# Flamingo block on one core: who splits the query weights in the prologue, and when ScalarE loads its sigmoid table

## The reference

```python
q = (layernorm(x) @ Wq.T) * scale;  k = ctx @ Wk.T;  v = ctx @ Wv.T
scores = sigmoid(q . k) per head;   o = (scores @ v) @ Wo.T
x = x + tanh(g_xattn[0]) * o
h = gelu(layernorm(x) @ w1 + b1);   y = h @ w2 + b2        # per expert
x = x + tanh(g_ffn[0]) * y
```

## Time and profile before

| | us |
|---|---|
| median of 3 runs | 1730.21 |
| lowest and highest | 1726.27, 1733.91 |
| profiled execution, own time | 1730.66 |
| its span in the profile | 1729.0 |
| PE busy | 1697.4 |
| DVE busy, ACT busy, POOL busy | 690.2, 776.6, 210.3 |

### The profile page before, as it was taken

How to read it: one execution, slowest core, us unless ns; L and a number is a source line. 1 busy time by engine, 2 the same in 40 slices (tenths; PEclk the granted TensorE clock), 3 DMA queues, 4 the chain that set the end, 5 groups by cost and what they waited for, 6 DMA issues and landing times.

```text
span 1729.0 us, 34127 instructions
## 1 busy us (share of the span) xinstructions
PE 1697.4 (98%) x12442; PEld 1498.7 (87%) x12442; DVE 690.2 (40%) x1171; ACT 776.6 (45%) x1007; POOL 210.3 (12%) x303
## 2 busy tenths in 40 slices
PE   6999999999999999999999999899999999999999
PEld 6888888888888888888888888799999999999998
DVE  5323323323324224233133132455555464655553
ACT  5545545446445455455454454433333333334332
POOL 1111212112111112122121121000000000000000
PEclk9999999999999999999999999999999999999999
DMA  8767767676777677677676676545262535435351
GB/s 262 217 185 218 209 193 204 202 206 204 190 211 211 187 210 215 183 210 211 193 219 193 197 207 198 155 153 175 95 221 98 196 119 174 141 127 176 101 181 58
DMA packets 199674, 315.75 MB, mean 183 GB/s; under 512 B 25368, under 2 KB 152672, under 8 KB 199520
## 3 DMA queue, kind: packets, MB, share of 16 engines
q1 hardware_dynamic: 176176, 236.05, 48.3%
q0 software_dynamic: 23344, 77.68, 12.8%
HBM read 235.06 MB, written 78.58 MB: 181 GB/s over the span
## 4 chain that ended last, share of the span: by engine, by line
PE 91%; DMA 4%; ACT 2%; DVE 1%; issue 1%; SPq 1%; POOLq 0%; ACTq 0%; DVEq 0%
PE fill_ps L539 37%; PE scores_ps L704 18%; PE fill_ps L685 13%; PE scores_ps L571 9%; PE heads_ps L585 8%; PE heads_ps L685 5%; ACT probs L742 2%; DMA k_scr<-k_stage 1%; DMA ctx_raw<-ctxT_in 1%; PE fill_ps L644 0%; SPq L312 0%; DMA xnT<-stat_scr 0%; DMA q_scr<-q_stage 0%; DMA probs<-WKT_in 0%; PE scores_ps L539 0%
## 5 line engine op out<-in xcount | busy, mean ns | idle before, releaser
L742 ACT ACTIVATE probs<-scores_ps 125x1792 f32<-125x1792 f32 x192 | 320.1, 1667 | 110.0 <-PE heads_ps L585 66.2
L539 PE MATMUL fill_ps<-ctx_hl,wK 128*128 128x250 f32 x2304 | 310.6, 284 | 9.3 <-DVE wK L901 8.4
L704 PE MATMUL scores_ps<-ctx_hl,wK 128*128 128x448 f32 x1536 | 316.7, 362 | 0.4 <-ACT st_row L771 0.4
L539 PEld LDWEIGHTS fill_ps<-ctx_hl,wK 128*128 128x128 f32 x2304 | 284.5, 191 | 32.1 <-issue 28.8
L704 PEld LDWEIGHTS scores_ps<-ctx_hl,wK 128*128 128x128 f32 x1536 | 288.0, 188 | 20.5 <-issue 0.8
L539 PE MATMUL fill_ps<-wV,ctx_hl 128*125 128x512 f32 x1152 | 286.8, 398 | 0.0
L539 PEld LDWEIGHTS fill_ps<-wV,ctx_hl 128*125 128x125 f32 x1152 | 208.9, 186 | 49.9
L685 PE MATMUL fill_ps<-wQ,wV 128*128 128x448 f32 x1152 | 243.0, 365 | 0.0
L498 POOL DMA_DIRECT2D k_scr<-k_stage x192 | 139.4, 726 | 769.5 <-DVE k_stage L982 714.9
L685 PEld LDWEIGHTS fill_ps<-wQ,wV 128*128 128x128 f32 x1152 | 216.0, 188 | 16.9
L571 PE MATMUL scores_ps<-q_st,k_st 96*125 96x224 f32 x1536 | 203.5, 275 | 14.4 <-ACT probs L742 9.3
(11 more groups left out here) (82 smaller groups left out, 1328.3 us busy)
## 6 DMA issues: line engine op xcount, KB each, us to landing
k_st<-k_scr SPq DMA_DIRECT2D x576, 125.0 KB, 3.1
v_sb<-w_in SPq DMA_DIRECT2D x96, 512.0 KB, 4.6
k_scr<-k_stage POOLq DMA_DIRECT2D x192, 250.0 KB, 3.8
ctx_raw<-ctxT_in SPq DMA_DIRECT2D x48, 500.0 KB, 5.4
q_st<-q_scr SPq DMA_DIRECT2D x192, 112.0 KB, 3.1
k_stage<-w_in SPq DMA_DIRECT2D x32, 512.0 KB, 3.6
q_scr<-q_stage POOLq DMA_DIRECT2D x64, 224.0 KB, 3.9
x_ln<-x_in SPq DMA_DIRECT2D x16, 448.0 KB, 4.7
```

What stands on the lines that cost most here:

```text
L539: last = pe.matmul(out_, lhsT(kt, a), rhs(kt, c), start=(kt == 0 and t == 0), stop=(kt == KT - 1 and t == 2))
L704: last = pe.matmul(y_ps[:, dt, 0:T], w2[:, slot, a, k, dt * P:(dt + 1) * P], hid_hl[:, slot, d, k, :], start=(c == 0 and k == 0 and t == 0 ...
L742: nc.scalar.activation(probs[0:ST, s % 3], scores_ps[0:ST, :, 0:2 * L], ACT.Sigmoid, scale=SCALE).then_inc(s_probs, 1)
```

## The change

The prologue is changed in five places. The low parts of the two query halves (n = 2, 3) are computed by POOL, right after the identity matrix, and have a semaphore of their own, `s_wq_lo`; PE and the first sigmoid wait for that where they need the query halves. DVE's counter `s_w_lo` counts the other six halves, in the order 0, 1, 4, 5, 6, 7 (`w_los` translates). DVE's list has half 4 in step 1 (where half 2 was) and half 5 in step 2 (where halves 3 and 4 were). ACT's list has the copies of halves 4 and 5 both in step 2, where half 5 was in step 3. And the tanh of the gates goes from step 11 to step 5, followed by a sigmoid of two columns, whose result lands in a tile (`x_mr`) that is overwritten before it is read.

```diff
--- before.py
+++ after.py
@@ -81,8 +81,9 @@
     BANK_LAST = {("O", 0): 0, ("O", 1): 1, ("U", 0): 2, ("U", 1): 3, ("S", 0): 0}
 
 
-    W_HI = {2: (4,), 3: (5,), 7: (6,), 8: (7,)}
-    W_LO = {1: (2,), 2: (3, 4), 3: (5,), 7: (6,), 8: (7,)}
+    W_HI = {2: (4, 5), 7: (6,), 8: (7,)}
+    W_LO = {1: (4,), 2: (5,), 7: (6,), 8: (7,)}
+    BY_POOL = (2, 3)
     CTX_HI = {5: 2}
     CTX_LO = {4: 1, 5: 2}
     CTX_SPLITS = {6: 0, 7: 1, 8: 2}
@@ -128,6 +129,10 @@
     def tile_of(i):
 
         return i - 4 if i >= 6 else i
+
+    def w_los(n):
+
+        return n if n <= BY_POOL[0] else n - len(BY_POOL)
 
     def attends(b):
         return not isinstance(b, int) or 0 <= b < B
@@ -251,7 +256,7 @@
             return ctx_hl[:, c, a].rearrange("p t s -> p (t s)")
 
         s_w_in = [sem(f"w_in{r}") for r in range(2 * len(w))]
-        s_w_hi, s_w_lo = sem("w_hi"), sem("w_lo")
+        s_w_hi, s_w_lo, s_wq_lo = sem("w_hi"), sem("w_lo"), sem("wq_lo")
         s_ctx_in = [sem(f"ctx_in{r}") for r in range(2)]
         s_ctx_hi, s_ctx_lo = sem("ctx_hi_s"), sem("ctx_lo_s")
         s_x_in, s_xr_in, s_g_in, s_gate = sem("x_in"), sem("xr_in"), sem("g_in_s"), sem("gate_s")
@@ -482,6 +487,11 @@
             nc.gpsimd.affine_select(out=ident[:], in_=ident[:], compare_op=ALU.not_equal, fill=1.0, base=0,
                                     pattern=[[-1, P]], channel_multiplier=1).then_inc(s_ident, 1)
 
+            for n in BY_POOL:
+                pool.wait_ge(s_w_hi, n + 1)
+                part = w["KQVO"[n // 2]][:, :, (n % 2) * KT // 2:(n % 2 + 1) * KT // 2, :]
+                nc.gpsimd.tensor_tensor(part[:, LO], w_raw_3d[n], part[:, HI].bitcast(F32), ALU.subtract).then_inc(s_wq_lo, 1)
+
             def store_q(b, i):
                 n, r = target(b, "Q", i), i % 2
                 alone(pool, done["Q"], nth("Q", b, i))
@@ -534,7 +544,10 @@
 
                 for kt in range(KT):
                     if halves is not None and kt % (KT // 2) == 0:
-                        pe.wait_ge(s_w_lo, halves + 2 * kt // KT + 1)
+                        if halves == BY_POOL[0]:
+                            pe.wait_ge(s_wq_lo, 2 * kt // KT + 1)
+                        else:
+                            pe.wait_ge(s_w_lo, w_los(halves + 2 * kt // KT) + 1)
                     for t, (a, c) in enumerate(TERMS):
                         last = pe.matmul(out_, lhsT(kt, a), rhs(kt, c), start=(kt == 0 and t == 0),
                                          stop=(kt == KT - 1 and t == 2))
@@ -632,7 +645,7 @@
                     if i == 0:
                         pe.wait_ge(s_o_lo, KT * b)
                         if known(b, 1):
-                            pe.wait_ge(s_w_lo, 8)
+                            pe.wait_ge(s_w_lo, w_los(8))
                     last = three_terms(ps[0:LT, :], lambda kt, a: oT[:, a, kt, i * LT:(i + 1) * LT],
                                        lambda kt, a: w["O"][:, a, kt, :])
                 elif kind == "S":
@@ -738,7 +751,8 @@
                 at(act, s_av, STEPS * b + s - 2)
                 if known(b, 0) and s == 0:
 
-                    act.wait_ge(s_w_lo, IN_PROBS)
+                    act.wait_ge(s_w_lo, w_los(IN_PROBS))
+                    act.wait_ge(s_wq_lo, len(BY_POOL))
                 nc.scalar.activation(probs[0:ST, s % 3], scores_ps[0:ST, :, 0:2 * L], ACT.Sigmoid,
                                      scale=SCALE).then_inc(s_probs, 1)
 
@@ -784,7 +798,7 @@
                 at(act, s_av, STEPS * (n - 1))
                 if known(n, 1) and i == 0:
 
-                    act.wait_ge(s_w_lo, 2 * len(w))
+                    act.wait_ge(s_w_lo, w_los(2 * len(w)))
                 nc.scalar.copy(v_sb[0:ST, place, tile_of(i), :], fill_bank(b, "V", i)[0:ST, :]).then_inc(done["V"], 1)
 
             def body(b, h, par):
@@ -806,9 +820,12 @@
                             w_hi(n)
                         if s in CTX_HI:
                             ctx_hi(0, 0, 0, CTX_HI[s])
-                        if s == 11:
+                        if s == 5:
                             act.wait_ge(s_g_in, 32)
                             nc.scalar.activation(gate[:], g_in[:], ACT.Tanh).then_inc(s_gate, 1)
+
+
+                            nc.scalar.activation(x_mr[:, 0, 0:2], g_in[:], ACT.Sigmoid)
                     elif s in CTX_SPLITS and prepares(b):
                         ctx_hi(b + 1, nh, npar, CTX_SPLITS[s])
                     if s == 5 and attends(b) and prepares(b):
```

## The result

| | before | changed |
|---|---|---|
| median of 10 runs each, us | 1728.89 | 1736.24 |
| lowest and highest | 1724.19, 1733.91 | 1732.0, 1741.64 |
| profiled execution, own time | 1730.66 | 1741.64 |
| its span | 1729.0 | 1740.0 |

The ratio is 1.0039, 95% interval [1.0025, 1.0053]: the changed kernel is slower by 6.7 us (4.3 to 9.2; the two medians are 7.35 us apart). The median 1736.24 is inside the range, and the runs can tell the difference from zero. The interval leaves out the forecast's +1.9 and has rival A's +5.9 in it.

The account below looks back on a forecast made before the run. PE, busy 98%, was taken to bound the kernel, so only the first 38 us counted. +2.07 - 0.18 = +1.9 us gave 1732.6 profiled and 1732.1 from the median; predicted 1732.5 us, range 1727 to 1740.

Parts of the forecast that it names:

- rival A: POOL's splits and DVE's small inverse-root steps exclude each other: x_ln +4.0, in all +5.9, 1736.3 us; chance 0.35.
- one of its own signs of being wrong: Prediction wrong if query matmuls start by 18 us, x_ln moves, or time changes behind 60 us.
- What bounds the kernel now: PE, busy 98% of 1729.0 us; it carries any shift of the first 38 us to the end.
- The query splits leave DVE, and value half 4 one step sooner: DVE's value split waits for ACT's copy and delays the xnT splits, so the first query matmul: +2.07 us.
- No wait inside Q0: Among the query matmuls PE no longer waits for the second query split: -0.18 us.
- What POOL pays: POOL's two splits take 2.26 us each, end at 16.0, and delay its queued stores 0.3 us at no cost.
- PE's clock: Half-clock stretch over the query matmuls stays the same length: 0 taken, ends -1.6 and up to +1 us.
- Value weights in one go: ACT's copy and DVE's split of value half 5 come at other places, neither gaining nor costing: 0.
- tanh and table: Earlier tanh, table load and small sigmoid on ACT: PE gains 0; ends 0 and -0.92 us.
- Rivals B and C: B: POOL's subtraction takes double, 4.5 us, 1741 us, chance 0.06; C: shorter round trip, full clock, 1729.6 us, chance 0.14.

Follow-up runs that it names:

- e1: Changed kernel with DVE's split of value half 4 put behind the xnT splits; 1.0015 against the kernel before.
- e2: Changed kernel with POOL's two splits waiting until x_ln is written; 1.0017 against the kernel before.
- e4: Changed kernel with e1's edit and POOL's splits released after the first two steps of the inverse root; 1.0023 against the kernel before.
- e8: Changed kernel with e1's edit and POOL's splits released at the end of the inverse root, beside x_ln; 1.0041 against the kernel before.
- e5: Changed kernel with the tanh back in step 11 and no small sigmoid; 1.0044 against the kernel before.
- e7: Kernel before with only the earlier tanh and the small sigmoid; 0.9999 against the kernel before.

## Why the prediction missed its size

The range held the measured median only because it had been drawn to take in rival A. The forecast's own mechanism failed at one step, and one of its own signs of being wrong came true: x_ln moved, from 14.74 to 18.44.

*What bounds the kernel now*: right, as far as the scatter lets one see. The shift arose before the second pair of scores (+7.49), and the timed difference (4.3 to 9.2) says that it was carried to the end.

*The query splits leave DVE, and value half 4 one step sooner* (+2.07): right. Between transposes and first query matmul it became +2.03 us, by the path named, with DVE's idle time in front of the value split released by ACT's copy. e1 takes it away, and 0.58 us more.

*No wait inside Q0* (-0.18): right; the 24 query matmuls are in one row.

*What POOL pays*: this is the step that failed. Its duration was right (2.26 us forecast, 2.34 to 2.38 measured), and so was the stretch (11.5 to 16.0 forecast, 10.92 to 15.60). But the step asked only who waits for POOL's results and what is queued behind them on POOL, and put its cost at nothing. What POOL's reading does to DVE in those 4.7 us was left to rival A, at a chance of 0.35 against 0.45. Measured it is +4.29 us, the largest term. e2 shows that it is POOL's doing, e4 and e8 that it follows POOL to other steps and to x_ln.

*Rival A* had the mechanism and the price, +4.0 for the exclusion. One detail of it was wrong: it let the two steps at L26 and L27 pass, for they have one tensor operand, and had the steps behind them held. The first two were held. By the rule of the Trainium skill (page "SBUF — State Buffer", section "Who interferes with whom") a `tensor_scalar` can be held as well, where it runs in a mode that uses both ports; the trace agrees with the outcome, 2.35 and 2.27 us, but no run shows in which mode these two steps of 4 elements ran. I had read the rule for two-operand instructions alone.

*PE's clock* (0 taken, ends -1.6 and +1): the size was off. Transposes +0.76, queries +0.79 with the vanished gap of 0.19 in it, so +0.98, values -0.29: +1.45 us together. I had looked at the wait ahead of the query matmuls only. x_ln's lateness put a second and longer wait (5.33 us) ahead of the transposes. PE stood still from 13.17, the clock fell near 16.0, in that wait, and was low until past 29.4. The transposes' +0.76 goes with it: they take 1.75 or 1.76 us in all five kernels with the late x_ln and at most 0.99 in the others. How much of the 0.98 over the queries comes of the change and how much is chance stays open: with x_ln as late, e1 had 0.03 there and e4 0.98. My price for the cold queries was low too. All 24 at half clock take 5.23 us (0.218 each), where I had 4.6 (0.192 each), from a stretch of 2.30 us whose 12 matmuls include those that its ends cut. Rival A's +5.9 with this term is 7.35, against 7.49 in the profile.

*Value weights in one go* and *tanh and table*, both 0: right. V1's copy was held a little (its start at 35.52 falls directly behind the small sigmoid), K9's was not: ACT still idled 0.60 us ahead of it. e5 and e7 show the zero for tanh and table from both sides.

*Rivals B and C*: POOL's split was not 4.5 us, and the clock did not help.

## What to carry to other kernels

An instruction put on an idle engine must be asked not only what waits for it but what it shuts out while it runs: in these runs POOL's subtraction, reading SBUF, held every DVE instruction without an operand in PSUM that started well before its end, and the price was up to POOL's whole instruction, however small the DVE instruction was. So a 2.3 us POOL instruction beside a chain of 0.2 us steps was the worst place for it, and beside DVE subtractions that read one operand from PSUM the best. And where two engines share a list order, an instruction moved up in one list takes its wait with it: look where what it waits for stands in the other list, and what is queued behind.

## What the runs showed of the hardware that I had not expected

- DVE instructions held beside a POOL subtraction of 1024 f32 elements (2.34 us): `tensor_scalar` with plain numbers on 4 elements (2.35 instead of 0.17 us), `tensor_scalar` with scalars from SBUF on 512 (2.56 instead of 0.54), `scalar_tensor_tensor` and `tensor_tensor` on 4 (2.26 and 2.25 instead of 0.16), `tensor_tensor` on 1024 with both operands in SBUF (3.19 instead of 1.23). Not held: `tensor_tensor` with one operand in PSUM (0.73 and 1.16, unchanged).
- At the seam of two POOL instructions in a row one waiting DVE instruction got through, and only one: the next was caught by the second (in the changed kernel, e1, e4, e5 and e8).
- `tensor_scalar` on 448 elements with a scalar from SBUF takes 0.449 us and on 4 elements 0.223, about half of the subtractions' price per element (e8's 2.56 us is this form, with two scalars).
- POOL was hardly lengthened (4.66 to 4.68 us for the two, 4.82 in e8), even where DVE always had something waiting.
- A profile's total scatters by 12 us (1685.8 to 1697.6) behind the prologue with the same program there, while the prologue repeats to a tenth where the clock comes back at the same place (e5's 35.70 us against 35.69) and to 1.2 us where it does not (e1 31.76, e8 32.85, e4 32.99).
- The granted clock came back to 1.00 inside the query matmuls in e1 and e8 and behind them in e4 (4.28, 4.99 and 5.23 us for the 24), though the transposes (1.75 to 1.76 us) and the wait ahead of the queries (1.33) were the same.
